# Graph layer 1: node counts beside the feature sums, placed by one set of fp32 one-hots

## The reference, cut to what matters

```python
h = jnp.maximum(_layernorm(x, axis=-1), 0.0)
# first layer
msgs = h[src]
summed = segment_sum(msgs, dst, num_segments=6250)        # 6250 x 128
counts = segment_sum(ones, dst, num_segments=6250)        # edges per node
agg = summed / jnp.maximum(counts, 1.0)[:, None]
out = agg @ W_l.T + h @ W_r.T + b
x = x + log_softmax(out, axis=1)
# second layer: messages weighted by an MLP of the edge features, summed by destination
```

## Time and profile before

| | us |
|---|---|
| median of 3 runs | 3466.1 (3463.45 to 3467.22) |
| span of the profiled execution | 3469.3 |
| of it: start and chunk 0 | 0 to 113 |
| chunks 1 and 2 | 113 to 178 |
| chunks 3 to 34 | 178 to 847 |
| chunks 35 and 36 | 847 to 889 |
| end of the loop | 889 to 910 |
| products of layer 1, and layer 2 | 910 to 3469 |

### The profile page before, as it was taken

How to read it: one execution, slowest core, us unless ns; L and a number is a source line. 1 busy time by engine, 2 the same in 40 slices (tenths; PEclk the granted TensorE clock), 3 DMA queues, 4 the chain that set the end, 5 groups by cost and what they waited for, 6 DMA issues and landing times.

```text
span 3469.3 us, 97235 instructions
## 1 busy us (share of the span) xinstructions
PE 2987.6 (86%) x26330; PEld 2437.6 (70%) x26331; DVE 2757.6 (79%) x7718; ACT 2085.3 (60%) x4907; POOL 1808.5 (52%) x1790
## 2 busy tenths in 40 slices
PE   0799999999668878899999989988889898998977
PEld 0699999999655556776766666766667666766766
DVE  8899999999786657777777777777777777777866
ACT  2599999998353335555555545555455555555656
POOL 3400010000127777667766676666766677677750
PEclk9999999999868889999999999999999999999999
DMA  3198888960103336666666656655666666666657
GB/s 117 37 326 313 311 309 310 311 213 3 38 19 107 103 103 172 179 175 160 178 164 161 160 150 172 166 162 147 166 168 180 165 158 184 173 158 175 181 154 207
DMA packets 506188, 593.04 MB, mean 171 GB/s; under 512 B 71050, under 2 KB 477058, under 8 KB 505905
## 3 DMA queue, kind: packets, MB, share of 16 engines
q1 hardware_dynamic: 449506, 470.49, 49.4%
q0 software_dynamic: 56400, 119.07, 9.9%
HBM read 293.94 MB, written 295.35 MB: 170 GB/s over the span
## 4 chain that ended last, share of the span: by engine, by line
DVE 36%; PE 32%; issue 17%; DVEq 7%; DMA 4%; POOL 2%; ACT 1%; SPq 0%; POOLq 0%; ACTq 0%
PE PS L1119 11%; DVE X L1017 8%; PE PS L1110 5%; DVE big L990 4%; PE PS L1282 4%; PE PS L1249 4%; DMA messages<-big,idxr 4%; DVE big L978 3%; DVE aux L768 3%; DVEq L1012 3%; DVE big L964 2%; DVE big L975 2%; DVE big L967 2%; DVE hpar L1006 2%; PE PS L1261 2%
## 5 line engine op out<-in xcount | busy, mean ns | idle before, releaser
L605 POOL DMA_INDIRECT messages<-big,idxr x1664 | 1637.0, 984 | 720.8 <-issue 466.5
L1282 PE MATMUL PS<-big,hpar 128*128 128x128 f32 x5120 | 663.8, 283 | 163.7 <-DVE hpar L1006 128.7
L1282 PEld LDWEIGHTS PS<-big,hpar 128*128 128x128 f32 x5120 | 610.5, 195 | 223.1 <-DVE hpar L1006 181.2
L1432 ACT ACTIVATE big<-PS,b1c 128x512 f32<-128x512 f32 x416 | 286.0, 688 | 708.3 <-PE PS L1238 708.3
L1017 DVE TENSOR_TENSOR X<-X,PS 128x128 f32 x1280 | 368.7, 288 | 325.3 <-PE PS L1282 131.9
L1119 PE MATMUL PS<-h_parts,counts 128*128 128x258 f32 x3626 | 565.3, 296 | 0.0
L1359 ACT ACTIVATE counts<-PS 128x784 fp32r<-128x784 f32 x592 | 481.7, 825 | 93.9 <-PE PS L1110 85.6
L1249 PE MATMUL PS<-W2s,big 128*128 128x128 f32 x3328 | 500.8, 295 | 0.0
L1249 PEld LDWEIGHTS PS<-W2s,big 128*128 128x128 f32 x3328 | 419.0, 197 | 98.3 <-issue 98.3
L1119 PEld LDWEIGHTS PS<-h_parts,counts 128*128 128x128 f32 x3626 | 470.2, 191 | 0.2 <-ACT counts L1359 0.2
L1443 ACT ACTIVATE big<-PS 128x512 f32<-128x512 f32 x416 | 247.6, 595 | 347.2 <-PE PS L1261 339.4
(11 more groups left out here) (222 smaller groups left out, 3639.1 us busy)
## 6 DMA issues: line engine op xcount, KB each, us to landing
messages<-zeros SPq DMA_DIRECT2D x896, 193.5 KB
big<-messages SPq DMA_DIRECT2D x320, 516.0 KB
aux<-slot_rows SPq DMA_DIRECT2D x416, 128.0 KB
big<-in_edge_attr_dram SPq DMA_DIRECT2D x402, 128.0 KB
messages<-big,idxr POOLq DMA_INDIRECT x1664
X<-in_x_dram SPq DMA_DIRECT2D x12, 448.0 KB, 6.9
out_dram<-X SPq DMA_DIRECT2D x6, 448.0 KB
edge_places<-big SPq DMA_DIRECT2D x1, 2496.0 KB, 13.2
```

Source lines behind the costliest of these rows:

```text
L605: pool.indirect_dma_start(strm_d, bass.IndirectOffsetOnAxis(ap=idxr[:, n % U, j:j + 1], axis=0), outr[:, n % U, j, :], None).then_inc(S_sc ...
L1282: last = nc.tensor.matmul(to[:, r * C:(r + 1) * C], finhot[:, n % 2, r * 2 + q, :], fin[:, k, r, q * ROW:q * ROW + C], start=(q == 0), sto ...
```

## The change

The two columns of ones in `h0p` are parted. The row becomes 128 high, 1, 128 low, 0: two halves of 129. The sum of the halves then gives 128 feature sums and the count at once, in one reduce of 129 columns. `aggv` grows by a column; the copy of the count, the second one-hot, its tile `ohc`, `cntv` and the wait between go. The second product of `place` takes the count column of `aggv`, repeated 128 times by a step of zero, as its weights, and the fp32 one-hot of the first product as its moving operand: fp32 in place of bf16. `aggv_ready` counts one per block in place of two. POOL writes the ones and the zeros by two memsets in place of one, and `h0_low` and `h0_back` write and read the low parts one element further on.

```diff
-        aggv = sb("aggv", [P, 2, C], fp32)
+        aggv = sb("aggv", [P, 2, C + 1], fp32)
-        cntv = sb("cntv", [P, 2], fp32)
-        ohc = ohv[:, :, 1, :].bitcast(bf16)[:, :, 0:P]
...
-                nc.gpsimd.tensor_tensor(h0p[:, chunk(c), C:2 * C], H[:, chunk(c), :], resid[:, n % 2, :].rearrange("p (b c) -> p b c", c=C),
+                nc.gpsimd.tensor_tensor(h0p[:, chunk(c), C + 1:2 * C + 1], H[:, chunk(c), :], resid[:, n % 2, :].rearrange("p (b c) -> p b c", c=C),
                                         ALU.subtract).then_inc(S["h0_low"], 1)
...
-                nc.gpsimd.tensor_tensor(H[:, chunk(c), :], h0p[:, chunk(c), 0:C].bitcast(fp32), h0p[:, chunk(c), C:2 * C].bitcast(fp32), ALU.add).then_inc(S["h0_back"], 1)
+                nc.gpsimd.tensor_tensor(H[:, chunk(c), :], h0p[:, chunk(c), 0:C].bitcast(fp32), h0p[:, chunk(c), C + 1:2 * C + 1].bitcast(fp32), ALU.add).then_inc(S["h0_back"], 1)
...
-            nc.gpsimd.memset(h0p[:, :, 2 * C:HW].bitcast(fp32), 1.0).then_inc(S["h0p_ready"], 1)
+            nc.gpsimd.memset(h0p[:, :, C:C + 1].bitcast(fp32), 1.0).then_inc(S["h0p_ready"], 1)
+            nc.gpsimd.memset(h0p[:, :, 2 * C + 1:HW].bitcast(fp32), 0.0).then_inc(S["h0p_ready"], 1)
...
-                nc.vector.tensor_reduce(aggv[:, h, :], psD[:, h, 0:2 * C].rearrange("p (a c) -> p c a", a=2), AX, ALU.add)
-                nc.vector.tensor_copy(cntv[:, h:h + 1], psD[:, h, 2 * C:2 * C + 1]).then_inc(S["aggv_ready"], 1)
-                nc.vector.tensor_scalar(ohv[:, h, 0, :], iotaF[:, :], nid[:, ds(c2, 1), h], None, ALU.is_equal)
-                dve.wait_ge(S["aggv_ready"], q * 2 + 1)
-                nc.vector.tensor_scalar(ohc[:, h, :], iotaF[:, :], nid[:, ds(c2, 1), h], cntv[:, h:h + 1], ALU.is_equal, op1=ALU.mult)\
-                    .then_inc(S["aggv_ready"], 1)
+                nc.vector.tensor_reduce(aggv[:, h, :], psD[:, h, :].rearrange("p (a c) -> p c a", a=2), AX, ALU.add)
+                nc.vector.tensor_scalar(ohv[:, h, 0, :], iotaF[:, :], nid[:, ds(c2, 1), h], None, ALU.is_equal).then_inc(S["aggv_ready"], 1)
...
-                pe.wait_ge(S["aggv_ready"], q * 2 + 2)
+                pe.wait_ge(S["aggv_ready"], q + 1)
                 wait(pe, S["agg_done"], q)
-                nc.tensor.matmul(psR[:, 0, :], aggv[:, h, :], ohv[:, h, 0, :], start=True, stop=True)
-                nc.tensor.matmul(psR[:, 1, :], onesb[:, :], ohc[:, h, :], start=True, stop=True).then_inc(S["sums_done"], 1)
+                nc.tensor.matmul(psR[:, 0, :], aggv[:, h, 0:C], ohv[:, h, 0, :], start=True, stop=True)
+                nc.tensor.matmul(psR[:, 1, :], aggv[:, h, C:C + 1].to_broadcast([P, P]), ohv[:, h, 0, :], start=True, stop=True).then_inc(S["sums_done"], 1)
```

More of the change, by code:

```diff
@@ L1116, in dense @@
                     pe.wait_ge(S["counts_out"], (q + 1) * OPB)
-                    wait(pe, S["aggv_ready"], (q - 1) * 2)
+                    wait(pe, S["aggv_ready"], q - 1)
                 for b in range(BPO * (o - 1), min(NB, BPO * o)):
@@ L1135, in layer0 @@
                         if known and c == 0 and h == 1 and o == 1:
-                            pe.wait_ge(S["h0p_ready"], 1)
+                            pe.wait_ge(S["h0p_ready"], 2)
                             pe.wait_ge(S["h0_high"], NCH)
```

## The result

The change made the kernel slower: 3493.6 us median (3488.15 to 3495.38) against 3464.8 us (3461.95 to 3467.22) of the kernel before on the same chip, a ratio of 1.0082, 95% interval 1.0068 to 1.0096, so +28.8 us where -12.9 was forecast. The range, 3442 to 3464, does not hold it. The spans of the two profiled executions are 3486.3 and 3469.3 us, 17.0 apart. (That of after belongs to the fastest run of after, that of before is longer than any timed run of before; the traces account for the 17.0, and what more the medians show is treated with the first experiment.)

A forecast was written before the change was run, and what follows sets the result against it. One loop of PE and DVE bounds the first layer: PE's own work plus one stall per block. Savings of 11.6 us (68 blocks) and 1.3 us (chunks 1 and 2) make -12.9, so 3453.2 us; range 3442 to 3464.

The forecast's parts named there:

- The second layer's 2559 us only move.: Everything behind the first layer: it starts at another time but keeps its length, so it adds nothing to the sum.
- block_sums: DVE, lines 776 to 780, per block: copy and scaled one-hot go, saving 0.33 us; the two instructions left take 0.53.
- The count pair: PE, line 1127, per block: the fp32 count product takes 0.22 us where bf16 took 0.06, adding 0.16.
- the second rival: Line 1127: loads of the repeated weights not hidden, pair 0.60 us, 3479.1 us in all; slower from 0.39 on; chance 0.08.
- PE's stall: PE's wait once per block for DVE's one-hot of line 768 falls from 0.49 to about 0.16 us.
- The sum of the first layer: Chunks 3 to 36, 68 blocks at -0.17 us, give -11.6; chunks 1 and 2 give -1.3; total -12.9 us.
- the first rival: ACT cannot follow PE, so only chunks 1 and 2 gain: 3464.8 us; chance 0.10.
- the third: The count pair costs nothing, hidden under the next octet's loads: gain 23.8 us, 3442.3 us; chance 0.05.
- DVE's wait for the place: DVE's wait in add_block, line 788, grows by up to 0.16 us per block and costs nothing.
- The last block: Its open chain: DVE's 0.33 us saved and the count pair's addition at PE's lower clock cancel; 0, ends -0.2 and +0.2.
- POOL's memsets: POOL at the start: two memsets for one, at most 0.19 us more, covered by DVE's wait for ACT's zeroing; 0.
- POOL's adds: Seven reads of the shifted low parts, line 524, 2.08 us each: taken as 0, bounds 0 and 14.6 us more.

The follow-up runs named there:

- the first experiment: The changed kernel plus 32 one-element memsets on DVE between the two layers: 3457.0 us against 3463.95 for the kernel before, ratio 0.9980.
- 0 and 128 memsets: The changed kernel with no added memsets, 3493.6 us, and with 128 one-element memsets on DVE between the layers, 3486.6 us in one run.
- another fifth loop: The changed kernel with the second layer's fifth loop cut into 6 rounds of 2 rings, not 3 of 4, plus 122 memsets: 3457.4 us, ratio 0.9972.

## Why the prediction was wrong

**The step that failed** is the last sentence of the sum: "The second layer's 2559 us only move." They do not only move. Their code is the same, but it lies 32 places earlier in DVE's stream and 26 later in PE's, and that cost more than the first layer gained. Of the 29.4 us lost behind the first layer in the traces, 23.4 and 5.2 come from DVE's blocks (loops 6 and 7) and 6.9 lie in the third loop, where kernels that differ in PE's stream alone show 4 to 7; the rest is -6.1, for which no cause was shown. It was a term that the sum put at nothing without naming what holds it there, and none of the rivals was about it.

The profile of before had what was needed. Its list of DMA queues shows 139 and 143 packets of instructions, and DVE's list of waits in its third loop shows such stops at work already:

```profile
q8 instruction: 143, 2.34, 0.3%
q14 instruction: 139, 1.14, 0.1%
```

```profile
DVE X L1017 <- issue: 21.6, 32, 0.7
...
DVE big L964 <- issue: 12.0, 7, 4.2
```

From there an estimate was to be had: loops 6 and 7 return to their heads five times and show no stop, the third loop's longest one is 4.2 us, so a shift of DVE's stream could cost about 5 x 4.2 = 21 us in these two, more than the whole gain. It would have been short by a quarter: they lost 28.6 us, since a stop there is up to 5.6 us and the step behind it runs slower too.

The Trainium skill has the rule that spoke against this change, in "Runtime: NRT & Kernel Launch", Instruction fetch mechanics: instructions come in blocks through a queue of the engine's own, and a taken branch whose target is not in the blocks held must wait for a fetch. The traces agree, with 19.2 us of such waits in the sixth loop. That page of the Trainium skill gives 16 KB blocks of 256 instructions, of which most engines hold two and TensorE more; PE's packets are of that size (2.34 MB in 143), DVE's are half of it (1.14 MB in 139), and its period of 128 was measured. With blocks of 256, two shifts that are 128 apart could not both have stopped a loop of 304, as 0 and 128 memsets did.

**Point by point.** *block_sums*: 0.54 us where 0.53 was forecast. *The count pair*: 0.23 us where 0.22 was; its loads lie under other work, so the second rival, the slower one, did not happen: its sign came, its mechanism did not. Its point of decision, 0.39 us, is far away. *PE's stall*: 0.17 us a block instead of 0.16. *The sum of the first layer*: -12.4 us at the last add, where -12.9 was forecast, and that this is so close is luck. In the loop a block gained 0.14 us instead of 0.17: the stall gave 0.32 for 0.33 and the pair took 0.17 to 0.18 for 0.16, so 68 blocks gave 9.6 us instead of 11.6. What was missing came from POOL's adds, which the sum had at nothing. *ACT*: its waits shrank to 18.4 us in the list and PE never waits for it, so the first rival fell; the third fell with the pair's 0.23. *DVE's wait for the place*: 19.4 us instead of 7.4 over the layer, at no cost, as argued. *The last block*: its add now starts 1.35 us after its place instead of 1.04, with DVE ahead of it 0.33 us shorter; the two cancel, as forecast:

```profile
895.32 0.80 PE L1121 MATMUL PS<-ohv,aggv 128*128 128x128 f32 x2 [9.79 <-DVE ohv L776]
895.90 0.63 PE L1122 MATMUL PS<-ohv,aggv 128*128 128x128 f32 x2
896.67 0.42 DVE L783 TENSOR_TENSOR big<-big,PS 128x256 f32 x1 [1.41 <-PE PS L1122]
```

*POOL's memsets*: no cost; DVE's wait for ACT's zeroing in chunk 1 is 9.8 us as before. *POOL's adds*: the bounds had "nothing" as their better end, and that was wrong. The view by line, after:

```profile
L522 POOL TENSOR_TENSOR hpar<-h_parts x7: 1769/1774/1793, 162.6 to 890.9; 128x896 f32<-128x896 f32 x7
```

They take 1.77 us instead of 2.08, and the one-hot beside the first three 6.00 instead of 6.93: about 0.9 us gained in chunk 2. The prediction read the other four as lying beside no busy DVE. They do hold it: at the end of the loop they run beside DVE's last work on the slots, whose instructions there take 0.2 to 0.3 us alone. The timelines of POOL and DVE, before and then after:

```profile
896.23 8.55 POOL L524 TENSOR_TENSOR hpar<-h_parts 128x896 f32<-128x896 f32 x4
896.27 2.10 DVE L833 SCALAR_TENSOR_TENSOR halves<-halves,extra 128x48 f32<-128x48 f32 x1
```

```profile
885.31 7.32 POOL L522 TENSOR_TENSOR hpar<-h_parts 128x896 f32<-128x896 f32 x4
887.18 1.81 DVE L828 SCALAR_TENSOR_TENSOR halves<-halves,extra 128x48 f32<-128x48 f32 x1
```

Four DVE instructions are held in either kernel, 8.1 us in all before and 6.9 after: 1.2 us more gained, which with the 0.33 of block_sums makes up the 1.5 us behind the 72nd add. Without these 2.1 us of POOL's the first layer would have gained some 10.3 us.

**What stays open.** The fourth loop took 359.9 to 365.7 us, once 376.6, with none to three stops of PE in it, and not the same number in two traces of the kernel before (one and two); its length does not follow them. Why the third loop took 370.5 with another fifth loop was not tried. Nor was a cause for the first loop, which stays at 240.0 while it fetches. The stretch between the layers takes 126.6 us after, and 130.7 and 136.5 in two traces of the kernel before, so the 4.1 us there are not shown to come of the change.

## What to carry to other kernels

An edit that adds or removes instructions moves every hardware loop behind it in the stream of each engine whose count it changes; where a loop's code fits the engine's fetch blocks only from some places, that is a term of the sum, however far from the edit. Count the instructions per engine ahead of the loops, look in the trace of before for idle time put down to "issue" at the heads of rounds and for packets on the instruction queues, and estimate the term as the number of returns times the longest such stop (here that gave 21 of 28.6 us). When a result is off, cut the trace by loop and compare stretches with equal work first: here a pad of 32 small instructions told in one run what no argument about the first layer could.

## What the runs showed of the hardware

- DVE's code comes in packets of 8 KB (1.14 MB in 139), and a loop of 304 instructions stops or not by its start modulo 128. A stop at the head of a round is 4.8 us on average (19.2 us in 4); the loop gets 23.4 us longer, 5.9 per return, since the step behind a stop is slower too.
- The stops take TensorE's clock with them: PE stands idle 4.6 to 5.7 us in each, and behind it the granted clock is at 0.50, the lower level, for 3.4 to 6.8 us. In the sixth loop the mean is 0.95 of the higher level instead of 1.00, and the same 1806 matmuls are busy 224.2 us instead of 215.9.
- Loading weights that are read with a step of zero costs what it costs for ordinary fp32 ones. The view by line of the count product's loads, after:

```profile
L1122 PEld LDWEIGHTS PS<-ohv,aggv x148: 190/192/333, 121.7 to 895.9; 128*128 128x128 f32 x148
```

  against 190 ns of median for the ordinary product, before as after.
- A POOL fp32 add is 15% shorter (1774 instead of 2080 ns) when its second operand starts 129 elements behind the first and not 128, with rows 258 apart in both. The adds of the low parts before the loop, which write to the moved place and do not read it, take 2077 ns in both kernels. No run tells why.
